# A graph attention layer on one core: the residual behind the first stage, a quarter of the columns folded by TensorE, other groups of row blocks

## The reference

```python
h = jnp.maximum(_layernorm(x, axis=-1), 0.0)
# in the layer, with x = h:
h = (x @ W.T).reshape(n, H, D)
s_src = jnp.einsum('nhd,hd->nh', h, a_src)
s_dst = jnp.einsum('nhd,hd->nh', h, a_dst)
attn = s_src[:, None, :] + s_dst[None, :, :]
attn = attn + adj_matrix[:, :, None] * We[:, 0] + be
attn = jnp.where((adj_matrix > 0)[:, :, None], attn, -jnp.inf)
attn = jax.nn.softmax(jax.nn.leaky_relu(attn, 0.2), axis=1)
h_out = jnp.einsum('ijh,jhd->ihd', attn, h).reshape(n, H * D)
return h_out + x @ Wr.T + br
# and the layer's result is added to the original x
```

## Time and profile before

| | us |
|---|---|
| runs | 2314.66, 2308.79, 2309.33, median 2309.33 |
| profiled execution | 2312.84 |
| its span, first to last instruction | 2310.8 |
| busy: DVE, POOL, ACT, PE | 2024.3, 1595.9, 1115.5, 1002.1 |
| stage 1, to the first deal of lists | 264.5 |
| DMA engines' busy share, mean | 67% |
| mean granted TensorE clock | 0.69 of full |

### The profile page before, as it was taken

How to read it: one execution, slowest core, us unless ns; L and a number is a source line. 1 busy time by engine, 2 the same in 40 slices (tenths; PEclk the granted TensorE clock), 3 DMA queues, 4 the chain that set the end, 5 groups by cost and what they waited for, 6 DMA issues and landing times. The chain is left out here.

```text
span 2310.8 us, 22965 instructions
## 1 busy us (share of the span) xinstructions
PE 1002.1 (43%) x3773; PEld 789.3 (34%) x3774; DVE 2024.3 (88%) x5351; ACT 1115.5 (48%) x4803; POOL 1595.9 (69%) x2020
## 2 busy tenths in 40 slices
PE   4767304522453194236332643353253336363343
PEld 3555203322432173225321532242242225242232
DVE  5899797899699789999888999999999998887942
ACT  2333205633574384446543654545354446485553
POOL 5544476777776777677777777777677774777775
PEclk9998656766675667667765766666666667676676
DMA  6444876667466757877777777777778885667333
GB/s 148 161 148 138 290 229 160 200 213 236 131 212 213 223 159 235 251 236 228 219 218 222 225 254 229 249 250 247 247 256 242 257 249 174 203 197 217 88 76 65
DMA packets 164570, 473.62 MB, mean 205 GB/s; under 512 B 35888, under 2 KB 54360, under 8 KB 164216
## 3 DMA queue, kind: packets, MB, share of 16 engines
q1 hardware_dynamic: 86088, 278.11, 36.6%
q0 software_dynamic: 78336, 194.09, 30.6%
HBM read 435.24 MB, written 36.83 MB: 204 GB/s over the span
## 5 line engine op out<-in xcount | busy, mean ns | idle before, releaser
L626 POOL DMA_INDIRECT arena<-table,arena x1262 | 1270.7, 1007 | 479.2 <-issue 322.1
L1347 PE MATMUL banks<-arena,ident 128*128 128x264 f32 x1566 | 500.2, 492 | 1161.9 <-DVE arena L939 1161.9
L1215 ACT ACTIVATE arena<-arena 128x32 f32<-128x32 f32 x3832 | 819.3, 307 | 2.2
L1347 PEld LDWEIGHTS banks<-arena,ident 128*128 128x128 f32 x1566 | 385.0, 251 | 1273.7 <-issue 1050.9
L772 DVE FIND_INDEX8 work<-work,adj_sb 128x8 uint32<-128x502 f32 (+56 forms) x775 | 667.2, 865 | 0.0
L783 DVE MAX8 work<-adj_sb 128x8 f32<-128x502 f32 (+56 forms) x775 | 652.4, 856 | 0.0
L1209 ACT ACTIVATE arena<-pre 128x104 f32<-128x104 f32 (+22 forms) x81 | 23.3, 304 | 910.1 <-DVE pre L929 909.6
L1353 PE MATMUL banks<-arena,ident 128*128 128x264 f32 x958 | 254.4, 408 | 42.5 <-ACT arena L1215 42.5
L939 DVE TENSOR_TENSOR arena<-arena 128x1024 f32<-128x1024 f32 (+8 forms) x169 | 226.4, 1389 | 51.3 <-ACT arena L1209 51.2
L1353 PEld LDWEIGHTS banks<-arena,ident 128*128 128x128 f32 x958 | 181.7, 197 | 103.6 <-ACT arena L1215 76.2
L1192 ACT ACTIVATE pre<-arena,we_all 128x13 f32<-128x13 f32 (+26 forms) x536 | 165.3, 406 | 87.3 <-DMA arena<-lists 87.0
(11 more groups left out here) (130 smaller groups left out, 966.2 us busy)
## 6 DMA issues: line engine op xcount, KB each, us to landing
adj_sb<-in_adj_dram SPq DMA_DIRECT2D x505, 512.0 KB, 4.4
arena<-table,arena POOLq DMA_INDIRECT x1262, 3.8
table<-arena POOLq DMA_DIRECT2D x32, 264.0 KB, 2.7
arena<-in_x_dram SPq DMA_DIRECT2D x32, 256.0 KB, 2.9
resid<-arena POOLq DMA_DIRECT2D x32, 256.0 KB, 2.6
out_dram<-arena POOLq DMA_DIRECT2D x32, 256.0 KB, 2.8
adj_sb<-in_adj_dram SPq DMA_DIRECT2D x1, 1536.0 KB, 23.5
lists<-arena,rank POOLq DMA_INDIRECT x67, 3.9
```

The source lines that it names most:

```text
L626: pool.indirect_dma_start(gath[0:n, un.slot(k), :], None, table[:, :], bass.IndirectOffsetOnAxis(ap=rec[0:n, k, 0:1], axis=0)).then_inc(la ...
L1215: last = s.activation(g, g, ACT.Copy, scale=gath[:, un.slot(k), HD + h:HD + h + 1])
L1347: last = m.matmul(ps_sum[:, u % 2, :], ident[:, :], gath[:, un.slot(k), :], start=(k == 0), stop=False)
```

## The change

The residual leaves stage 1. ScalarE keeps mean and deviation of all rows; x is loaded a second time, 128 rows at a time, and in 64 steps ScalarE makes relu(layernorm) in one activation, TensorE turns it, ScalarE copies it back, TensorE sums x, br and the product with Wr in PSUM, ScalarE copies that out and issues both stores. 32 steps stand before unit 0's exps, 16 behind unit 0's weights, 16 and two that drain behind unit 1's (`RES_AT`). Their buffers are the last 10 slots of the ring, which now has 85 and is held at 75 for its first four laps (300 slots, `LAPS`). In stage 1 GpSimd only stores the table; the ranks of tile 0 are begun two rounds before its end.

From tile 7 on TensorE folds the columns 6144 to 8191 onto 4096 to 6143: an identity times the near ones plus 2**-64 times the far ones, in four PSUM banks of 512. VectorE scans these banks as four segments and then the left half (4096 columns); `unfold` tells near from far by size and corrects places and values. ScalarE counts the nonzeros of either part by two Sign passes with a sum (`see_fold`), and a tile whose counts differ from what was found is flagged. Pieces of the right half are now loaded first, and wait for `see_fold` of the tile two before.

The groups are 3, 4, 8, 10, 11, 11, 10 and 6 tiles instead of 3, 4, 8, 8, 8, 8, 8, 8, 4 and 4; the slots are 1240. Finds are due earlier: 31 sources by unit 11 (26 before), 67 by unit 52 (60 by 45, 67 by 60).

```diff
-GSLOTS = 86
+GSLOTS = 85
 LANES = 4
+LAPS = (75, 75, 75, 75)
+RES_AT = (32, 16, 16)
...
-          (16, (29, 20, 18, 16, 15, 14, 13, 11)),
-          (24, (25, 17, 15, 14, 13, 12, 11, 9)),
-          (32, (22, 15, 14, 13, 12, 11, 10, 8)),
-          (40, (23, 15, 13, 12, 10, 9, 8, 7)),
-          (48, (23, 13, 12, 11, 10, 9, 8, 7)),
-          (56, (20, 11, 9, 8)),
-          (60, (18, 11, 9, 7)))
-SEGS = {1: (35, 2.3), 2: (26, 2.0), 3: (19, 2.0), 4: (17, 1.9), 8: (14, 2.1), 14: (12, 1.8), 16: (9, 2.0), 24: (9, 2.1), 32: (7, 2.0),
-        48: (7, 1.6)}
-FOUND = ((0, 7), (11, 26), (45, 60), (60, 67))
+          (16, (29, 20, 18, 17, 16, 15, 14, 13, 12, 10)),
+          (26, (24, 17, 15, 14, 14, 13, 12, 11, 11, 9, 8)),
+          (37, (23, 15, 14, 13, 12, 11, 10, 10, 9, 8, 7)),
+          (48, (23, 14, 12, 11, 10, 10, 9, 8, 7, 6)),
+          (58, (18, 12, 10, 9, 8, 7)))
+SEGS = {1: (35, 2.3), 2: (26, 2.0), 4: (17, 1.9), 7: (10, 1.8), 11: (8, 1.9), 13: (7, 1.8),
+        23: (8, 1.8), 28: (6, 1.8), 33: (5, 1.7)}
+FOLD_FROM = 7
+FOLD_AT = N // 2
+FOLD = N // 4
+BANK = 512
+BANKS = FOLD // BANK
+TURNS = (1, 1, 0, 0, 0, 1, 0, 0, 0, 0, 0, 0, 0, 0, 0, 2, 0, 0, 1, 0, 0, 0, 0, 0, 0, 1, 0, 0, 1, 0,
+         0, 1, 0, 0, 0, 3, 0, 0, 0, 1, 0, 0, 0, 0, 0, 0, 0, 0, 0, 0, 0, 0, 0, 0, 0, 0, 0)
+FOLD_SCALE = 2.0 ** -64
+FOLD_SPLIT = 2.0 ** -32
+FOLD_TINY = 2.0 ** -120
+FOUND = ((0, 7), (11, 31), (36, 56), (52, 67), (58, 67))
...
+    laps = LAPS
     at, owner, part_sums, acts, issued = 0, [None] * GSLOTS, 0, 0, NV + 1
     for un in units:
-        un.ring = at
+        un.cells = []
+        for _ in range(un.K):
+            un.cells.append(at)
+            at += 1
+            if at == (laps[0] if laps else GSLOTS):
+                at, laps = 0, laps[1:]
         un.free_at = [owner[un.slot(k)] for k in range(un.K)]
...
-        ps_hd = banks[:, 2:6, 0:ROW + H].rearrange("p (u b) n -> p u b n", u=2)
-        ps_res = banks[:, 6:8, :].rearrange("p u (b n) -> p u b n", b=2)
-        ps_w, ps_w2 = banks[:, 6, :], banks[:, 7, :]
+        ps_turn, ps_res = banks[:, 3, 0:HD], banks[:, 7, 0:HD]
+        ps_hd = banks[:, 3:7, 0:ROW + H].rearrange("p (u b) n -> p u b n", u=2)
+        ps_w, ps_w2 = banks[:, 7, :], banks[:, 2, :]
+        ps_fold = banks[:, 4:4 + BANKS, :]
+        ps_rank, ps_above = banks[:, 2, 0:RANKS], banks[:, 2, 512 - KLIST - 1:512]
...
-            sp.dma_start(br_all, br.partition_broadcast(P)).then_inc(S["small_in"], 16)
+            sp.wait_ge(S["rest_zero"], 1)
+            sp.dma_start(br_row, br.rearrange("(a n) -> a n", a=1)).then_inc(S["small_in"], 16)
...
+                    if sources[c - 2].folded and n * PIECE >= FOLD_AT:
+                        sp.wait_ge(S["fold_seen"], sources[c - 2].fold + 1)
+                    else:
+                        sp.wait_ge(S["scanned"], segs_before[c - 2] + scans_of(sources[c - 2], n))
+                    if i >= 2:
+                        sp.wait_ge(lane, 16 * (loads_before(so) * (PIECES // 2) + i // 2))
                     sp.dma_start(adj_sb[:, b, cols], load_adj(so.t)[:, cols]).then_inc(lane, 16)
...
+            pool.memset(rest, 0.0).then_inc(S["rest_zero"], 1)
...
-                    pool.wait_ge(S["res_done"], u + 1)
-                    nc.gpsimd.tensor_tensor(rt_sb[:, q, :, :], rt_sb[:, q, :, :],
-                                            br_all.unsqueeze(1).to_broadcast([P, 2, HD]), ALU.add
-                                            ).then_inc(S["br_added"], 1)
-                    pool.wait_ge(S["br_added"], u + 1)
-                    pool.dma_start(by_unit(resid, u), rt_sb[:, q, :, :]).then_inc(S[f"res_out{q}"], 16)
-                    pool.dma_start(by_unit(out, u), rt_sb[:, q, :, :]).then_inc(S[f"res_out{q}"], 16)
-            for b in range(2):
-                for q, each in (("hd_out", 16), ("res_out", 32)):
-                    pool.wait_ge(S[f"{q}{b}"], each * (UNITS // 2))
-
-            pool.wait_ge(S["pad_out"], 16)
...
+                    if un.free_at[k] is None and un.cells[k] == LAPS[0]:
+                        pool.wait_ge(S["res_out0"], 32 * UNITS)
+                        pool.wait_ge(S["res_out1"], 32 * UNITS)
...
             load_dealt(groups[0])
+            for q in range(2):
+                pool.wait_ge(S[f"hd_out{q}"], 16 * (UNITS // 2))
+            pool.wait_ge(S["pad_out"], 16)
+            pool.wait_ge(S["s_done"], UNITS)
...
-                if u >= 2:
-                    dve.wait_ge(S[f"res_out{q % 2}"], u // 2 * 32)
-                for b in range(2):
-                    last = v.scalar_tensor_tensor(out=rt_sb[:, q % 2, b, :], in0=ps_res[:, q % 2, b, :],
-                                                  scalar=rstd[:, q, b:b + 1], in1=x_sb[:, q, b, :],
-                                                  op0=ALU.mult, op1=ALU.add)
-                last.then_inc(S["res_done"], 1)
-                dve.wait_ge(S["res_done"], u + 1)
-                dve.sem_inc(S["x_free"], 1)
...
+                def segment(s):
+                    if s < so.banks:
+                        return ps_fold[:, s, :]
+                    return a[:, bounds[s - so.banks]:bounds[s - so.banks + 1]]
...
+            def unfold(so):
+                f = so.fold
+                vf, jf = val8[:, 0:8 * BANKS], jpad[:, 0:8 * BANKS]
+                v.tensor_scalar(fold_tag[:, :], vf, FOLD_SPLIT, 1.0 / FOLD_SCALE, ALU.is_lt, ALU.mult
+                                ).then_inc(S["tagged"], 1)
+                v.tensor_scalar(fold_one[:, 0, :], vf, FOLD_SPLIT, 0.0, ALU.is_ge, ALU.add,
+                                accum_out=fold_found[:, 0, f:f + 1])
+                v.tensor_scalar(fold_one[:, 1, :], vf, 0.0, 0.0, ALU.is_gt, ALU.add,
+                                accum_out=fold_found[:, 1, f:f + 1])
+                dve.wait_ge(S["jshift"], so.c + 1)
+                dve.wait_ge(S["tagged"], f + 1)
+                cut = 8 * (BANKS - so.turn)
+                for lo, hi, far in ((0, cut, FOLD + BANK * so.turn), (cut, 8 * BANKS, BANK * so.turn)):
+                    if hi > lo:
+                        last = v.scalar_tensor_tensor(out=jf[:, lo:hi], in0=fold_tag[:, lo:hi],
+                                                      scalar=float(far << JBITS) * FOLD_SCALE, in1=jf[:, lo:hi],
+                                                      op0=ALU.mult, op1=ALU.add)
+                v.scalar_tensor_tensor(out=vf, in0=fold_tag[:, :], scalar=1.0, in1=vf, op0=ALU.max, op1=ALU.mult
+                                       ).then_inc(S["unfolded"], 1)
+                dve.wait_ge(S["unfolded"], f + 1)
...
+            def load_again(r):
+                act.dma_start(xr_sb[:, r % 3, :], x[bass.ts(r, P), :]).then_inc(S[f"xr_in{r % 3}"], 16)
+            def residual_step(r):
+                if r < TILES:
+                    act.wait_ge(S[f"xr_in{r % 3}"], 16 * (r // 3 + 1))
+                    if r >= 2:
+                        act.wait_ge(S["hr_turned"], r - 1)
+                    s.activation(hr[:, r % 2, :], xr_sb[:, r % 3, :], ACT.Relu, bias=shift[:, r // 2, r % 2:r % 2 + 1],
+                                 scale=rstd[:, r // 2, r % 2:r % 2 + 1]).then_inc(S["hr_done"], 1)
+                if 1 <= r <= TILES:
+                    act.wait_ge(S["hr_turned"], r)
+                    if r >= 3:
+                        act.wait_ge(S["res_ps"], r - 2)
+                    s.activation(hrT[:, (r - 1) % 2, :], ps_turn, ACT.Copy).then_inc(S["hrT_done"], 1)
+                if r >= 2:
+                    act.wait_ge(S["res_ps"], r - 1)
+                    if r + 1 < TILES:
+                        load_again(r + 1)
+                    if r >= 4:
+                        act.wait_ge(S[f"res_out{r % 2}"], 32 * (r // 2 - 1))
+                    s.activation(rt_sb[:, r % 2, :], ps_res, ACT.Copy).then_inc(S["res_copied"], 1)
+                    act.wait_ge(S["res_copied"], r - 1)
+                    act.dma_start(out[bass.ts(r - 2, P), :], rt_sb[:, r % 2, :]).then_inc(S[f"res_out{r % 2}"], 16)
+                    act.dma_start(resid[bass.ts(r - 2, P), :], rt_sb[:, r % 2, :]).then_inc(S[f"res_out{r % 2}"], 16)
...
+            def see_fold(so):
+                act.wait_ge(S["folded"], BANKS * (so.fold + 1))
+                for side in range(2):
+                    cols = adj_sb[:, so.buf, FOLD_AT + FOLD * side:FOLD_AT + FOLD * (side + 1)]
+                    last = s.activation(cols, cols, ACT.Sign, bias=tiny[:, :],
+                                        accum_out=fold_counts[:, side, so.fold:so.fold + 1])
+                last.then_inc(S["fold_seen"], 1)
+            act.wait_ge(S["tiny_set"], 1)
+            for r in range(3):
+                load_again(r)
+            act.wait_ge(S["shifted"], 1)
             prepare(units[0])
+            for r in range(RES_AT[0]):
+                residual_step(r)
+            seen = 0
             for un in units:
                 if un.u + 1 < len(units):
                     prepare(units[un.u + 1])
```

(52 more changed lines are left out.)

## The result

The changed kernel takes 5038.3 us in the median of its runs (5008.9 to 5051.6), the kernel before 2311.0 beside it: a ratio of 2.178, 95% interval 2.168 to 2.188. The forecast was 2325, with 2390 as the upper end. Two separate things were wrong in it, and the profile shows them apart.

What follows compares the result with a forecast made beforehand. GpSimd's gathers, 1.35 us each, were taken as the bound: 242 to the first gather + 433 to unit 5 + 1625 to the last gather + 26 tail = 2326 us of span. Forecast 2325 us, 0.7% slower; range 2250 to 2390.

Steps and rivals of the forecast that it cites:

- the segments stay 14: VectorE's folded find: the number of segments stays 14, in a find priced at 21.4 us.
- s: Cost of one of the residual's steps on ScalarE, taken as 3.4 us, set by the load of x landing in 2.5.
- the loop through PSUM: Bound on one residual step: four matmuls 1.9, handovers, issue and copy; 3.2 us at the low clock, 2.3 at the high.
- upper end of 5.3: Highest residual step considered: 5.3 us, a landing of 4.4 us like the adjacency's pieces, plus 0.9 of activations.
- 74 + 66 s + 135 us: First gather to unit 5's gathers: ScalarE's queue, then five finds and the softmax chain; 433 us at s = 3.4.
- The start: First gather at 242 us, 39 earlier: 33 less for VectorE's residual instructions, 2 more for a memset.
- The rest: Unit 5's start to the last gather's end: 1625 us against 1685, from fewer gathers, no store waits, fewer list loads.
- The fold's terms: Per tile: TensorE 4 to 8 us, ScalarE's two Sign passes 1.7 each, both covered; VectorE's find 3 us shorter.
- A: Rival, faster: residual step cheap at 2.9 us, start 236, five finds of 20; time 2279 us; chance 0.35.
- B: Rival, no change: load of x lands in 2.3 us, step 3.2, time 2311 us; chance 0.13.
- C: Rival, much slower: contention on the DMA engines, a landing of 3.5 makes the step 4.4, 2390 us; chance 0.18.
- D: Rival: PSUM reads or TensorE waits eat the fold's 4.3 us; chain moves 14 us, 24 of store waits return; no own chance.

Runs made afterwards that it cites:

- e1: The changed kernel with the ten segments of tiles 7 to 10 cut by power 2.1 instead of 1.8, so no flag: 2470.3 us, 1.070 of the kernel before.
- e2: e1 with tile 10 cut into eight segments by power 1.9, so that it alone is flagged and redone: 3330.1 us, 1.439 of the kernel before.
- e3: The changed kernel without flags, its residual steps without the matmuls that add x and the bias: 2383.9 us, 1.030 of the kernel before.
- e8: e4 with the 64 residual steps spread over the units, ring at 75 slots throughout, four output buffers, earlier stores: 2310.5 us, 0.997 of the kernel before.
- e6: The changed kernel without flags, residual made in the first stage again; fold, groups and ring of 85 stay: 2296.9 us, 0.991 of the kernel before.
- e4: The changed kernel with only tiles 60 to 63 folded and otherwise the segments of the kernel before, none flagged: 2457.7 us, 1.063 of the kernel before.
- e5: The kernel before with only the change's new groups and table of finds: 2296.0 us, 0.992 of the kernel before.
- e9: e8 with nothing folded, 85 slots for three laps, five output buffers, later stores, no residual step before unit 6: 2287.8 us, 0.987 of the kernel before.
- e10: e9 with three residual steps behind each of units 6 to 15 and two behind each of the next 17: 2281.6 us, 0.986 of the kernel before.

## Why the prediction was wrong, point by point

**The flags: a step that wasn't in it.** The prediction counted segments ("the segments stay 14") and priced them. It never asked what they are allowed to hold. The front of this document says that a dense path redoes flagged tiles and that none is flagged before; the change touches the very table that keeps them unflagged, and what follows could be counted from the inputs without a chip. No rival had it. The flags are 2568 of the 2727 us of loss (after against e1), shown by e1 and e2.

**The size of a step, s.** Forecast 3.4, measured 5.30, which is (5.3 - 3.4) x 66 = 125 us. The term that failed is the loop through PSUM: "four matmuls 1.9". The step has four matmul calls (x, the bias, two for Wr); the row behind the price shows four instructions, and they are two calls. Counted right, that row gives 3.8 + 0.9 for copy and handovers, 4.7; measured were 4.35 and 0.95. So this loop, and not the load of x, sets the step. The text's upper end of 5.3 is the same number by chance: it was a landing of 4.4 us, and it stood in no rival and not in the range.

**In sum,** e1, the main part alone, has a span of 2460 us where 2326 were forecast: 11 less in the start, 117 more to unit 5, 28 more in the rest.

**The frame around s held.** The text gave the first folded find's end and the chain behind it as 74 + 66 s + 135 us behind the first gather. With s = 5.30 this is 559; measured 565 in the kernel after, with its 13 longer steps, and 550 in e1, with its five short ones. That it lies between is partly luck. The mechanism (ScalarE's queue, the exps behind it, slots, ranks) is as forecast: the exps of unit 0 came at 409 us (357), VectorE stood 85 us ahead of its first scan from PSUM (forecast 50), GpSimd waited 173.4 us for sums (over 60) and 59.5 for the ranks (30). e3 shows that the step's cost reaches the end, e8 and e6 that it is the place of the steps and not their work. e4 corrects one link: of VectorE's 85 us for the first folded find only 10 to 20 count, for the wait for exps would end at the same time.

**The start.** Forecast 242, measured 229.8. The first deal and the first gather of the kernel after, in GpSimd's timeline:

```profile
215.71 1.07 POOL L698 DMA_INDIRECT lists<-arena,rank  x1 [0.31 <-issue]
...
229.77 1.00 POOL L673 DMA_INDIRECT arena<-table,arena  x1 [3.71 <-issue]
```

From the first deal to the first gather it is 14.1 us (16.6 taken); the other 10 of the 12 us are stage 1, which got shorter than by the two instructions counted. The change also moves the count and the ranks of the first lists into the last units of stage 1, and the text didn't price this move; whether it gave the 10 us stays open.

**The rest.** Forecast 1625 from unit 5 to the last gather, measured 1645 (1653 in e1). The store waits went as forecast (2.9 us left). 20 to 28 us were lost to what the text held covered: gathers waited 159 us for landings of earlier ones, against 109; 36 of the 50 us lie behind unit 5. e5 and e6 (110 and 162 us) and e4 and e1 (116 and 176) put this beside the fold, but e9 and e10, which fold nothing and spread the residual's transfers, have it too (157 and 151). Its cause stays open. The new groups also gave 23 us and not 30 when alone (e5).

**The fold's terms.** TensorE's share was 8.9 us a tile in e1 (260 and 249 us for 57 tiles), forecast 4 to 8; ScalarE's two passes 1.99 us each, forecast 1.7. Both are past the forecast; TensorE's was mis-sized as the step was, since eight calls a tile are 16 instructions. They weren't wholly covered: VectorE waited some 77 us for folds in e6 (28 times), which it paid from its slack. Its own saving was 2.9 us a tile in e6 against e5, forecast 3, and that it is worth nothing at the end was right: e6 against e5 (2296.9 and 2296.0) and the rest of e1 against e4 (1653 and 1645).

**The rivals.** A and B needed a step of 3.2 us and less and fall; even at the high clock, A's own condition, the short steps of e1 took 3.3 us. C, contention, had the right side and, in the main, the wrong cause: 4.4 us a step and 2390. In the kernel after the loads of x landed in 2.1 us in the median, below the 2.5 taken, and the steady 5.3 us come from TensorE; late loads made 13 steps longer, 16 us in all. D, the fold worth nothing, was true and small, as it said.

The Trainium skill (DMA: Bandwidth & Descriptors, Anatomy of one DMA) gave 2.3 us for 128 KB; its fit is for DMAs that GpSimd issues, and these are ScalarE's. The trace comes near it where the steps stand in a block (the loads 2.1 us, the two stores 2.1 and 2.7), and doesn't where they are spread among gathers: there the loads land in 4.7 and the two stores in 4.2 and 5.6 us.

```profile
arena<-in_x_dram ACTq DMA_DIRECT2D x64, 128.0 KB, 4.7
out_dram<-arena ACTq DMA_DIRECT2D x64, 128.0 KB, 4.2
resid<-arena ACTq DMA_DIRECT2D x64, 128.0 KB, 5.6
```

(e10; count, KB each, median us from issue to landing.)

## What to carry to other kernels

Where a fast path has an escape, ask of every table in a diff what keeps the escape from being taken, and count it on the inputs; price one taking of it (860 us in e2) before any gain in the fast path. Price an operation that is moved on the engine that takes it, in instructions as the trace counts them and not in calls. And before crediting a wait that goes, look at what ends at the same moment: 85 us of waiting were worth 10 to 20 (e4), and 36 us of waiting on the bound engine came back as waits for landings (e6).

## What the runs showed of the hardware

A transfer of very small pieces is two thirds of a redone tile: some 570 of 860 us. The rearranged table is 256 KB, 65536 numbers of 4 bytes, moved nearly one number a packet; in the stretch 2455 to 3000 us of the kernel after the DMA engines were busy and moved next to nothing:

```profile
DMA packets 64978, 4.48 MB, mean 8 GB/s; under 512 B 64848, under 2 KB 64848, under 8 KB 64848
...
q1 hardware_dynamic: 64976, 4.45, 92.3%
```

That is 256 KB in 570 us, and most of the 4.48 MB is the adjacency's block at its start. With 16 engines it makes 16 x 570 / 64848 = 0.14 us a packet and engine, an estimate from these rows. The Trainium skill (DMA: Bandwidth & Descriptors, Specifications) asks for at least 512 B a transfer for the full rate; this stretch has nothing near that size but fits it: it moved 8 GB/s, the adjacency's block included. Each fp32 matmul call is two instructions in these traces, and a transpose one (L1493, two calls, x2). Reading PSUM costs VectorE next to nothing more: a scan of 512 columns from there takes 685 ns (busy us, mean ns of one; kernel after), one of 502 columns from SBUF 667 ns in the kernel before.

```profile
L829 DVE MAX8 work<-banks 128x8 f32<-128x512 f32 x228 | 148.1, 685 | 165.0 <-PE banks L1561 165.0
```
